# Reordering SyncE's transfers in a fused attention and mixture-of-experts layer: last group's strips first, next rows last

## The chip, the cores and the metric

The kernel runs on one core of a Trainium2 chip. The metric is device time in microseconds of one execution, the median over runs. Engines are named as the profile names them: PE (TensorE), PEld (its weight loads), DVE (VectorE), ACT (ScalarE), POOL (GpSimd) and SP (SyncE). SP computes nothing here: it issues DMA transfers, in one fixed order.

## The reference

One layer in float32 over x of 8 x 1024 tokens by 256 features:

```python
xn = layernorm(x)
x = x + attention(xn, w_qkv, w_out) + moe(xn, wg, w1, b1, w2, b2)
# attention: 16 heads of 64, causal, softmax over 1024 keys, then the output projection
qkv = einsum('bse,ehd->bshd', xn, w_qkv); q, k, v = split(qkv, 3, axis=-1)
logits = einsum('bqhd,bkhd->bhqk', q, k) / sqrt(64); probs = softmax(where(tril, logits, neg))
out = einsum('bshd,hde->bse', einsum('bhqk,bkhd->bqhd', probs, v), w_out)
# moe: 8 experts, top 2, 2048 slots per expert, relu(x w1 + b1) w2 + b2, weighted by the two gates
```

## The kernel before

The program has three stages: layernorm and router, the experts (results go to memory, one row for each slot), and from about 908 us of the profiled span on `attention_and_sum`, which also adds the experts' rows. Only that stage is changed.

**Units and steps.** The work of attention is 64 units: 8 batches (`BATCH`) of 8 pairs of heads (`PAIRS`). The order of each engine's work is written out by tables over 20 steps of a unit (`STEP_OF`, `ACT_STEP`, `DVE_STEP`, `RUN_STEP`, `POOL_AT`). In unit n, PE makes the scores of unit n in five rounds of query tiles (L1231), the projections of q and k for unit n+1 (L1142) and of v (L1157), the output projections "o0" to "o3" of unit n-1 (L1176), and the products of probabilities and values (L1263) in three runs: groups 0 and 1 at step 3 of unit n+1, group 2 at step 7 of unit n+1 (24 matmuls), group 3 at step 15 of unit n+1 (32 matmuls). A group is 256 query rows.

**Turning the probabilities.** Groups 0 and 1 are transposed by PE. For groups 2 and 3 DVE turns blocks of 32x32 into `squares` (L1398), and DMAs bring these blocks to their places in `pT`: 16 strips a group and unit, of which SP issues 12 (`place`, L1085: 96 KB each for group 2, 128 KB for group 3) and POOL 4 (`place_rest`, L1465, at steps 16 and 5). `place(n, g)` waits for the squares of the unit and for the PE run that read `pT` of this group a unit earlier. PE's run of group 2 or 3 waits for all 16 strips.

**The residual rows.** `res` holds the 1024 rows of a batch. It is filled from x (`refill`, L1094, four parts of 256 KB, one for each group), DVE adds each unit's output projection into it (L1381), POOL the rows of the experts (`total`, L1500, one tile of 128 rows a unit, at step 4), and at the end of a batch it is stored (`store`, L1089, four parts). Unit n with n % 8 == 0 is the change of batch: in it DVE adds the previous batch's last projections, o0 at step 6, o1 at 10, o2 at 12, and o3 at step 2 of the unit after. `store(b-1, g)` waits for that addition, `refill(b, g)` for the store of the same part. The new rows are first needed in unit n+1: part 0 by POOL's `total` at step 4, and by DVE's o0 at step 6.

**SP's other loads.** `load_w(n+2)` (L1073, two DMAs of 128 KB into `wr`) waits until POOL has split the weights of the unit before (`wlo`, L1448, step 1); POOL reads the new ones at step 1 of unit n+1 (L1441). The tile of tokens `xnt` (L1110, 128 KB) is loaded once PE has transposed the last one (step 1), and PE reads it at step 1 of unit n+1. `load_wv` (L1077, two DMAs of 128 KB into `wvr`) comes in even units once POOL has split the last ones (L1458, step 17), and is read two units later.

SP waits in order: an instruction behind a wait is issued after it, whatever it is for. Before, a unit's order is: `load_w`, `xnt`, strips of group 3 of unit n-1, [stores 0 to 2, refills 0 to 2], strips of group 2 of unit n, `load_wv`, [store 3, refill 3]; what stands in brackets is there at a change of batch alone, seven times in all.

Of the kernel before, what the change touches and what calls it, by code (L numbers as in the profile page):

```python
# [845 lines left out]
def attention_and_sum(nc, k, x, xn_dram, w_qkv, w_out, pick, y_dram, out, start):  # L846
# [7 lines left out]
    GROUPS = SEQ // GQ  # L854
# [77 lines left out]
    class Pieces:  # L932
        def __init__(self, sem_, own):
            self.sem, self.value, at = sem_, {}, 0
            for n in range(-1, UNITS + 1):
                for _, p in pieces(n):
                    at += own(p)
                    self.value[n, p] = at
# [5 lines left out]
    with ExitStack() as c:  # L944
# [45 lines left out]
        with ExitStack() as pre:  # L990
# [7 lines left out]
            @block.sync  # L998
            def _(e):
                e.dma_start(wo_raw, wov).then_inc(s_wo, 16)  # L1000
# [63 lines left out]
        def strip(g, a, b):  # L1064

            to, of = slice(b * BL, (b + 1) * BL), slice(a * BL, (a + 1) * BL)
            return wide[g][to, a].rearrange("p x r -> p (x r)"), sq[g][of, b].rearrange("p x k i -> p (x k i)")

        @block.sync
        def _(e):  # L1070
            def load_w(m):
                for c_ in range(MC):
                    e.dma_start(wr[:, 2 * c_:2 * c_ + 2], wv[m % PAIRS][:, c_, :, 0:2 * HDIM]).then_inc(wload.sem, 16)  # L1073

            def load_wv(m):
                for c_ in range(MC):
                    e.dma_start(wvr[:, c_], wvv[m % (PAIRS // 2)][:, c_, :, 2 * HDIM:]).then_inc(wvload.sem, 16)  # L1077

            def place(n, g):
                e.wait_ge(squared.sem, squared.at(n, 4 * g - 4))  # L1080
                if n > 0:
                    e.wait_ge(pv.sem, pv.at(n - 1, RUN_OF[g] + 1))
                for a in range(QUARTERS - 1):
                    for b in range(QUARTERS):
                        e.dma_start(*strip(g, a, b)).then_inc(placed[g].sem, 16)  # L1085

            def store(b, g):
                e.wait_ge(dve.sem, dve.at((b + 1) * PAIRS, f"o{g}"))
                e.dma_start(outv[:, b, 2 * g:2 * g + 2], res[:, 2 * g:2 * g + 2]).then_inc(stored[g].sem, 16)  # L1089

            def refill(b, g):
                if b > 0:
                    e.wait_ge(stored[g].sem, stored[g].at(b - 1, 16))
                e.dma_start(res[:, 2 * g:2 * g + 2], xv[:, b, 2 * g:2 * g + 2]).then_inc(rload[g].sem, 16)  # L1094

            e.dma_start(xnt[:], xnv[AHEAD]).then_inc(xload.sem, 16)
            load_w(1)
            load_wv(1)
            for n in range(UNITS):
                b, u = n // PAIRS, n % PAIRS  # L1100
                if n == 0:
                    e.wait_ge(s_wolo, 1)
                    for g in range(GROUPS):
                        refill(0, g)
                if n + 2 < UNITS:
                    e.wait_ge(wlo.sem, wlo.at(n, MC))
                    load_w(n + 2)
                if n + 1 + AHEAD < TILES:
                    e.wait_ge(filled.sem, filled.at(n, "xn"))
                    e.dma_start(xnt[:], xnv[n + 1 + AHEAD]).then_inc(xload.sem, 16)  # L1110
                if n > 0:
                    place(n - 1, 3)
                if b > 0 and u == 0:
                    for g in range(3):
                        store(b - 1, g)
                    for g in range(3):
                        refill(b, g)
                if n < UNITS - 1:
                    place(n, 2)
                if n % 2 == 0 and n // 2 + 2 < UNITS // 2:  # L1120
                    e.wait_ge(wvlo.sem, wvlo.at(n // 2, MC))
                    load_wv(n // 2 + 2)
                if b > 0 and u == 0:
                    store(b - 1, 3)
                    refill(b, 3)
            for g in range(GROUPS):
                store(BATCH - 1, g)
            for g in range(GROUPS):
                e.wait_ge(stored[g].sem, stored[g].at(BATCH - 1, 16))

        @block.tensor
        def _(e):
# [47 lines left out]
            def turn_p(n, name):  # L1180
                W, unit, at = work_bank(name), min(n, UNITS - 1), 0
                i, h, _, _ = TURNS[name][-1]
                e.wait_ge(scaled.sem, scaled.at(unit, SCALE_ORDER.index((i, h)) + 1))
                for i, h, k0, blocks in TURNS[name]:
                    for b in range(blocks):
                        cols = slice(OFFSET[i] + (k0 + b) * P, OFFSET[i] + (k0 + b + 1) * P)
                        ins = e.transpose(W[:, at * P:(at + 1) * P], room_of(unit, i, h)[:, cols], k["ident"][:])  # L1187
                        at += 1
                return ins

            def work(n, name):

                same = [(m, p) for m in (n - 1, n) if m >= -1 for _, p in pieces(m) if BANK_OF.get(p, 0) == BANK_OF[name]]
                same = same[:same.index((n, name))]
                if same:
                    m, p = same[-1]
                    if by_act(p):
                        e.wait_ge(act.sem, act.at(m, p))
                    if by_dve(p):
                        e.wait_ge(dve.sem, dve.at(m, p))  # L1200
                if name[0] == "p":
                    ins = project(n, name)
                elif name[0] == "v":
                    ins = values_of(n, name)
                elif name == "xn":
                    ins = turn_xn(n)
                elif name[0] == "t":
                    ins = turn_p(n, name)
                else:
                    ins = out_project(n, name)  # L1210
                ins.then_inc(filled.sem, 1)
# [359 lines left out]
```

## Time and profile before

| | us |
|---|---|
| median of 3 runs | 2915.8 (2915.28 to 2918.36) |
| the profiled execution's own time | 2915.7 |
| its span | 2913.9 |
| PE busy | 2814.5 (97% of the span) |
| DVE, ACT, POOL busy | 2084.7 (72%), 1699.7 (58%), 1723.0 (59%) |
| mean granted PE clock | 0.988 of full speed |
| chain that ended last: on PE | 66% of the span |

Times in rows are microseconds from the start of the span, unless marked ns. "x12" is a number of instructions; a time in square brackets is idle time of the engine before the instruction, with what ended it. "L1085" is a line of the kernel. A DMA's row on SP is the time to issue it, not to move its data; where a row gives the landing, that is from issue to the last byte. PEclk 1.00 is the full granted clock, the DMA share is the mean busy share of the core's 16 DMA engines.

### The profile page before, as it was taken

The numbers are of one execution on the slowest core, as the hardware profiler recorded it, in microseconds if no ns is written. First come the engines' busy times: TensorE is split into PE (matmuls) and PEld (weight loads), VectorE is DVE, ScalarE is ACT, GpSimd is POOL, SyncE is SP. The second block draws the span as 40 slices with busy tenths as digits, with TensorE's granted clock in tenths as the row PEclk, the third lists the DMA queues.
The fourth block names the chain that finished last, engine by engine and source line by source line (L and its number), as shares of the span: only waits on it lengthen the run. The fifth ranks groups of instructions, "written<-read, shape, count | busy, mean of one in ns | idle before, by whom it ended". The sixth has DMA issues, their size and how long they took to land.

```text
span 2913.9 us, 61264 instructions
## 1 busy us (share of the span) xinstructions
PE 2814.5 (97%) x21321; PEld 2284.1 (78%) x21321; DVE 2084.7 (72%) x4448; ACT 1699.7 (58%) x3934; POOL 1723.0 (59%) x2631
## 2 busy tenths in 40 slices
PE   5599999999998999999999999999999999999998
PEld 4489999899997777777777777777777777777776
DVE  7843444344434888888888888888888888888886
ACT  3454444445454666666666666666666666666664
POOL 3032122211212777777877877777777778777774
PEclk9799999999999999999999999999999999999999
DMA  7022212221212565665665565665665556556553
GB/s 241 29 82 75 69 52 83 76 68 47 82 54 74 141 158 144 163 154 145 168 150 145 147 170 147 157 166 142 157 164 151 149 146 176 141 145 183 136 134 93
DMA packets 248774, 371.58 MB, mean 128 GB/s; under 512 B 77392, under 2 KB 177744, under 8 KB 248480
## 3 DMA queue, kind: packets, MB, share of 16 engines
q1 hardware_dynamic: 216000, 276.31, 35.3%
q0 software_dynamic: 32480, 91.44, 11.7%
q8 instruction: 174, 2.85, 0.4%
q14 instruction: 120, 0.98, 0.1%
HBM read 102.80 MB, written 33.55 MB: 47 GB/s over the span
## 4 chain that ended last, share of the span: by engine, by line
PE 66%; DVE 1%; SPq 1%; DMA 0%; issue 0%; ACT 0%; POOL 0%; DVEq 0%; ACTq 0%
PE O L1263 18%; PE S L1231 16%; PE W L1142 12%; PE W L1157 7%; PE W L1176 7%; PE W L1187 6%; SPq L1085 1%; DVE pr L1355 0%; PE W L1165 0%; DMA pT<-squares 0%; DVE squares L1398 0%; ACT pr L1293 0%; DMA out<-res 0%; ACT pT L1283 0%; DVE res L1381 0%
## 5 line engine op out<-in xcount | busy, mean ns | idle before, releaser
L1436 POOL TENSOR_SCALAR pr<-pr,rinv 128x512 f32<-128x512 f32 (+7 forms) x1024 | 748.4, 744 | 399.7 <-DVE rinv L1361 398.6
L1293 ACT ACTIVATE pr<-pr,negm 128x512 f32<-128x512 f32 (+7 forms) x1024 | 787.3, 774 | 285.3 <-DVE negm L1355 285.3
L1355 DVE CUSTOM_DVE_ANT_0 pr<-S,late 128x512 f32<-128x512 f32 (+7 forms) x1024 | 717.0, 751 | 112.9 <-PE S L1231 112.9
L1263 PE MATMUL O<-pT,vv 128*64 128x256 f32 (+1 forms) x5120 | 541.3, 362 | 3.1 <-DMA pT<-squares 3.1
L1398 DVE STREAM_TRANSPOSE squares<-pr 128x640 f32<-128x640 f32 x504 | 494.8, 1020 | 0.0
L1263 PEld LDWEIGHTS O<-pT,vv 128*64 128x64 f32 x5120 | 346.4, 137 | 181.8 <-issue 20.4
L832 DVE TENSOR_TENSOR hl<-h,hh 128x512 fp32r<-128x512 f32 x256 | 192.3, 751 | 315.2 <-ACT hh L793 315.0
L789 ACT ACTIVATE h<-pH,b1c 128x512 f32<-128x512 f32 x256 | 175.9, 687 | 366.0 <-PE pH L719 334.1
L1283 ACT ACTIVATE pT<-W 128x512 f32<-128x512 f32 (+3 forms) x520 | 199.6, 437 | 215.8 <-PE W L1187 215.8
L731 PE MATMUL pY<-w2h,hh 128*128 128x256 f32 x1024 | 287.7, 281 | 2.5 <-DVE hl L832 2.5
L731 PE MATMUL pY<-w2l,hh 128*128 128x256 f32 x1024 | 289.1, 282 | 0.0
L731 PE MATMUL pY<-w2h,hl 128*128 128x256 f32 x1024 | 288.0, 281 | 0.0
L1465 POOL DMA_DIRECT2D pT<-squares x504 | 258.8, 521 | 0.3 <-issue 0.2
L1231 PE MATMUL S<-khf,qh 64*128 64x512 f32 (+2 forms) x1024 | 218.6, 422 | 3.6 <-DVE negm L1355 3.6
L1142 PE MATMUL W<-xnh,wh 128*128 128x512 f32 x512 | 215.1, 420 | 3.0 <-DVE klf L1389 1.5
L719 PE MATMUL pH<-xh,w1h 128*128 128x512 f32 x512 | 205.5, 401 | 4.2 <-DVE xl L804 2.6
L664 POOL COPY idx<-slot_token 128x4 uint32 (+1 forms) x30 | 8.8, 293 | 335.3 <-PE pX L705 335.3
L1142 PE MATMUL W<-xnl,wh 128*128 128x512 f32 x512 | 203.2, 397 | 0.0
L1142 PE MATMUL W<-xnh,wl 128*128 128x512 f32 x512 | 203.1, 397 | 0.0
L719 PE MATMUL pH<-xh,w1l 128*128 128x512 f32 x512 | 201.5, 394 | 0.0
L719 PE MATMUL pH<-xl,w1h 128*128 128x512 f32 x512 | 201.4, 393 | 0.0
L1381 DVE TENSOR_TENSOR res<-W,res 128x512 f32<-128x512 f32 x256 | 175.6, 686 | 35.6 <-PE W L1176 25.4
(176 smaller groups left out, 6479.6 us busy)
## 6 DMA issues: line engine op xcount, KB each, us to landing
pT<-squares SPq DMA_DIRECT2D x756, 128.0 KB
pT<-squares SPq DMA_DIRECT2D x756, 96.0 KB, 2.8
pT<-squares POOLq DMA_DIRECT2D x252, 128.0 KB
pT<-squares POOLq DMA_DIRECT2D x252, 96.0 KB, 3.0
y<-yb SPq DMA_DIRECT2D x128, 128.0 KB, 1.7
wr<-in_L_attn_w_qkv SPq DMA_DIRECT2D x128, 128.0 KB, 2.3
x<-in_L_attn_x SPq DMA_DIRECT2D x16, 512.0 KB, 8.9
xn<-xn SPq DMA_DIRECT2D x16, 512.0 KB, 4.4
```

The costliest lines, as they stand in the source:

```text
L719: ins = e.matmul(pH[hc % 4][:], w[par][:, m, ws], xx[q][:, m, :], start=(n == 0), stop=(n == 3 * MC - 1))
L731: ins = e.matmul(pY[t % 2][:], hs[q][:, hc, ts_], ws[par][:, hc, :], start=(hc == 0 and n == 0), stop=(hc == HC - 1 and n == 2))
L1142: ins = e.matmul(W, ws[:, 2 * m + of_k], xs[:, t0:t0 + HT, m, :], start=(i == 0), stop=(i == 3 * MC - 1))
L1157: ins = e.matmul(W[:, t * VW:(t + 1) * VW], xs[:, t0 + t, m, :], ws[:, m, :], start=(j == 0), stop=(j == len(terms) - 1))
L1176: ins = e.matmul(W[:, t * MODEL:(t + 1) * MODEL], os_[:, ts_], ws[:, of % PAIRS, :], start=(i == 0), stop=(i == 2))
L1231: ins = e.matmul(S[h][:, off + f * HALF:off + f * HALF + cols], t[hs, i * P:(i + 1) * P], u[f][n % 2][hs, 0:cols], start=(j == 0), stop=(j ...
L1263: ins = e.matmul(O[hs, o0 + a:o0 + GQ], vv[n // 2 % 2][:, kt, vs], turned_p, start=(kt == 0), stop=(kt == KT - 1))
L1293: e.activation(p, p, ACT.Exp, bias=negm[:, c0:c0 + 1], scale=-1.0, accum_out=rsum[:, c0:c0 + 1]).then_inc(expd.sem, 1)
L1355: e.tensor_tensor_reduce(room_of(n, i, h)[:, off:off + w], S[h][:, off:off + w], late[:, SEQ - w:], 1.0, -MASKED, ALU.add, ALU.min, negm[: ...
L1398: e.transpose(sq[g][:, :, 2 * h + i % 2, 0:KT, :], room_of(n, i, h)[:, OFFSET[i]:OFFSET[i] + KT * P].rearrange("p (k b i) -> p b k i", b=Q ...
L1436: e.tensor_scalar(p, p, rinv[:, c0:c0 + 1], 1.0, ALU.mult, ALU.mult).then_inc(scaled.sem, 1)
L1465: e.dma_start(*strip(g, QUARTERS - 1, b)).then_inc(pool_placed[g].sem, 16)
```

## The change

`place(n - 1, 3)` goes to the head of SP's loop. At a change of batch, refills 0 to 2 go behind the strips of group 2, and behind store 3, and store 3 and all four refills stand ahead of `load_wv`. No transfer is added, removed or resized, and no other engine's program is changed.

```diff
+                if n > 0:
+                    place(n - 1, 3)
                 if n + 2 < UNITS:
                     e.wait_ge(wlo.sem, wlo.at(n, MC))
                     load_w(n + 2)
                 if n + 1 + AHEAD < TILES:
                     e.wait_ge(filled.sem, filled.at(n, "xn"))
                     e.dma_start(xnt[:], xnv[n + 1 + AHEAD]).then_inc(xload.sem, 16)
-                if n > 0:
-                    place(n - 1, 3)
                 if b > 0 and u == 0:
                     for g in range(3):
                         store(b - 1, g)
-                    for g in range(3):
-                        refill(b, g)
                 if n < UNITS - 1:
                     place(n, 2)
+                if b > 0 and u == 0:
+                    store(b - 1, 3)
+                    for g in range(GROUPS):
+                        refill(b, g)
                 if n % 2 == 0 and n // 2 + 2 < UNITS // 2:
                     e.wait_ge(wvlo.sem, wvlo.at(n // 2, MC))
                     load_wv(n // 2 + 2)
-                if b > 0 and u == 0:
-                    store(b - 1, 3)
-                    refill(b, 3)
```

SP's queue at the first change of batch (unit 8 and the head of unit 9), before, from the refill of part 2 on. `pT2` and `pT3` are the places of groups 2 and 3, `s_stored3` is the landing of store 3:

```order
L1094 DMA res<-in_L0_attn_x 128x2x256 [waits s_stored2]
L1085 DMA pT2<-squares2 32x768 [waits s_pv,s_squared]
L1085 DMA pT2<-squares2 32x768 x11
L1077 DMA wvr<-in_L0_attn_w_qkv 128x4x64 [waits s_wvlo]
L1077 DMA wvr<-in_L0_attn_w_qkv 128x4x64
L1089 DMA out<-res 128x2x256 [waits s_dve]
L1094 DMA res<-in_L0_attn_x 128x2x256 [waits s_stored3]
L1073 DMA wr<-in_L0_attn_w_qkv 128x2x128 [waits s_wlo_a]
L1073 DMA wr<-in_L0_attn_w_qkv 128x2x128
L1110 DMA xnt<-xn 128x256 [waits s_filled]
L1085 DMA pT3<-squares3 32x1024 [waits s_pv,s_squared]
L1085 DMA pT3<-squares3 32x1024 x11
```

The same place of SP's queue with the change:

```order
L1085 DMA pT2<-squares2 32x768 [waits s_pv,s_squared]
L1085 DMA pT2<-squares2 32x768 x11
L1089 DMA out<-res 128x2x256 [waits s_dve]
L1094 DMA res<-in_L0_attn_x 128x2x256 [waits s_stored0]
L1094 DMA res<-in_L0_attn_x 128x2x256 [waits s_stored1]
L1094 DMA res<-in_L0_attn_x 128x2x256 [waits s_stored2]
L1094 DMA res<-in_L0_attn_x 128x2x256 [waits s_stored3]
L1077 DMA wvr<-in_L0_attn_w_qkv 128x4x64 [waits s_wvlo]
L1077 DMA wvr<-in_L0_attn_w_qkv 128x4x64
L1085 DMA pT3<-squares3 32x1024 [waits s_pv,s_squared]
L1085 DMA pT3<-squares3 32x1024 x11
```

Between the landing of store 3 and the strips of group 3 there stood refill 3, two `wr` loads and `xnt`; now there stand refill 3 and two `wvr` loads, and refills 0 to 2 are issued between store 3 and the wait for its landing.

An ordinary unit (the second after the change of batch), SP's queue before:

```order
L1073 DMA wr<-in_L0_attn_w_qkv 128x2x128 [waits s_wlo_a]
L1073 DMA wr<-in_L0_attn_w_qkv 128x2x128
L1110 DMA xnt<-xn 128x256 [waits s_filled]
L1085 DMA pT3<-squares3 32x1024 [waits s_pv,s_squared]
L1085 DMA pT3<-squares3 32x1024 x11
```

and with the change:

```order
L1085 DMA pT3<-squares3 32x1024 [waits s_pv,s_squared]
L1085 DMA pT3<-squares3 32x1024 x11
L1073 DMA wr<-in_L0_attn_w_qkv 128x2x128 [waits s_wlo_a]
L1073 DMA wr<-in_L0_attn_w_qkv 128x2x128
L1112 DMA xnt<-xn 128x256 [waits s_filled]
```

Twelve strips moved ahead of three loads.

## Rows read from the trace of the kernel before

**Rows 1.** The page: engines, slices of the span, costliest groups.
```profile
PE 2814.5 (97%) x21321; PEld 2284.1 (78%) x21321; DVE 2084.7 (72%) x4448; ACT 1699.7 (58%) x3934; POOL 1723.0 (59%) x2631
...
PE   5599999999998999999999999999999999999998
...
L1263 PE MATMUL O<-pT,vv 128*64 128x256 f32 (+1 forms) x5120 | 541.3, 362 | 3.1 <-DMA pT<-squares 3.1
```
**Rows 2.** Windows: busy time of a stretch, PEclk, DMA share, GB/s.
```profile
1010.40:1041.20 30.80, 30.80 (x248) 23.94 (x248) 25.77 (x58) 19.79 (x51) 23.26 (x37) 1.00 0.59 151
1195.00:1227.60 32.60, 30.84 (x247) 23.94 (x246) 25.81 (x58) 19.76 (x51) 23.55 (x38) 1.00 0.64 166
```
**Rows 3.** Waits of PE in 1160 to 1230, and in 1230 to 2850.
```profile
PE O L1263 <- DMA pT<-squares: 1.8, 1, 1.8
...
PE O L1263 <- DMA pT<-squares: 1.3, 1, 1.3
```
**Rows 4.** Timeline of SP at the first change of batch.
```profile
1172.83 7.95 SPq L1085 DMA_DIRECT2D pT<-squares  x12
1180.82 4.37 SPq L1089 DMA_DIRECT2D out<-res  x3
1185.43 3.49 SPq L1094 DMA_DIRECT2D res<-in_L_attn_x  x3
1189.02 7.59 SPq L1085 DMA_DIRECT2D pT<-squares  x12
1196.65 1.19 SPq L1077 DMA_DIRECT2D wvr<-in_L_attn_w_qkv  x2
1199.80 0.38 SPq L1089 DMA_DIRECT2D out<-res  x1
1204.11 0.37 SPq L1094 DMA_DIRECT2D res<-in_L_attn_x  x1
1204.53 0.98 SPq L1073 DMA_DIRECT2D wr<-in_L_attn_w_qkv  x2
1205.56 0.47 SPq L1110 DMA_DIRECT2D xnt<-xn  x1
1206.12 8.44 SPq L1085 DMA_DIRECT2D pT<-squares  x12
```
**Rows 5.** Chain of waits at PE's first wait in this stage.
```profile
1213.32 0.59 SPq L1085
1213.92 0.04 issue
1213.96 4.79 DMA pT<-squares
1218.76 0.04 issue
1218.80 1.29 PE O L1263 x9
```
**Rows 6.** Timeline of SP at the second, third and sixth change of batch.
```profile
1448.14 0.38 SPq L1089 DMA_DIRECT2D out<-res  x1
1451.36 0.37 SPq L1094 DMA_DIRECT2D res<-in_L_attn_x  x1
...
1696.04 0.38 SPq L1089 DMA_DIRECT2D out<-res  x1
1698.25 0.37 SPq L1094 DMA_DIRECT2D res<-in_L_attn_x  x1
...
2439.76 9.95 SPq L1085 DMA_DIRECT2D pT<-squares  x12
```
**Rows 7.** Timeline of PE: run of group 3 after the sixth change.
```profile
2452.75 1.08 PE L1263 MATMUL O<-pT,vv 128*64 128x256 f32 x8
```
**Rows 8.** Windows of 2 us after the first change's store 3, as rows 2.
```profile
1202.00:1204.00 2.00, 2.00 (x21) 1.86 (x18) 2.00 (x7) 0.20 (x1) 1.55 (x4) 1.00 0.04 8
1206.00:1208.00 2.00, 2.00 (x24) 1.42 (x22) 1.13 (x3) 1.38 (x6) 2.00 (x6) 1.00 0.83 247
1210.00:1212.00 2.00, 2.00 (x13) 1.69 (x13) 1.63 (x7) 2.00 (x6) 1.53 (x3) 1.00 1.04 270
```
**Rows 9.** Timeline of POOL and DVE after the first change of batch.
```profile
1205.00 0.73 POOL L1500 TENSOR_TENSOR res<-res,yg 128x256 f32<-128x256 f32 x1
...
1205.85 0.69 DVE L1381 TENSOR_TENSOR res<-W,res 128x512 f32<-128x512 f32 x1 [0.66 <-POOL res L1500]
1207.03 0.18 DVE L1361 RECIPROCAL rinv<-rsum 128x4 f32<-128x4 f32 x1 [0.48 <-ACT pr L1293]
1207.59 0.42 DVE L1405 TENSOR_TENSOR ol<-O,oh 128x256 fp32r<-128x256 f32 x1 [0.39 <-ACT oh L1324]
1208.88 0.96 DVE L1355 CUSTOM_DVE_ANT_0 pr<-S,late 128x768 f32<-128x768 f32 x1 [0.86 <-PE S L1231]
```
**Rows 10.** SP, DVE and POOL two units after the first change, and a unit later.
```profile
1234.78 0.89 SPq L1073 DMA_DIRECT2D wr<-in_L_attn_w_qkv  x2
1236.28 23.25 SPq L1085 DMA_DIRECT2D pT<-squares  x24
...
1232.34 2.36 DVE L1398 STREAM_TRANSPOSE squares<-pr 128x1024 f32<-128x1024 f32 x2
...
1262.75 0.39 POOL L1441 TENSOR_SCALAR wr<-wr 128x256 f32<-128x256 f32 x1
```
**Rows 11.** DMA issues of the page: kind, count, size, median time to landing.
```profile
wr<-in_L_attn_w_qkv SPq DMA_DIRECT2D x128, 128.0 KB, 2.3
...
res<-in_L_attn_x SPq DMA_DIRECT2D x32, 256.0 KB, 3.0
out<-res SPq DMA_DIRECT2D x32, 256.0 KB, 3.7
```

## The prediction

> **What bounds the kernel now.** I read the page first. PE is busy 97% of the span, and from the fourteenth slice on, the attention stage, its digit is 9 in nearly all [rows 1]. Then the windows: an ordinary unit of this stage takes 30.80 us and PE is busy for all 30.80 of it, at the full granted clock [rows 2]. A transfer can cost time here only where PE waits for it. So the third view is PE's own waits in the part of the stage that repeats. Between 1160 and 2850 us there are two, both of the run of values (L1263) for strips of pT, 1.8 and 1.3 us [rows 3]; the page's total for that line is the same 3.1 [rows 1]. The unit with the first wait lasts 32.60 us with 30.84 busy [rows 2]: the wait is time lost, not time shifted. These 3.1 us are all that a better order of SP's queue can return in that part, 0.11% of 2915.7. The start of the stage and the last unit have PE waits as well, but for other engines, and SP's order there hardly changes.
>
> Both waits stand one unit after a change of batch. The timeline of SP tells why [rows 4]. Store 3 is issued at 1199.80; SP then waits for it to land before it may issue refill 3 (1204.11), and only then come two wr loads, xnt, and at 1206.12 the twelve strips of group 3. The chain of waits at PE's stall goes through these strips: the last is issued at 1213.32 and waited for until 1218.76 [rows 5]. The wait of SP for the store was 4.3 us at the first change, 3.2 at the second (1451.36 less 1448.14) and 2.2 at the third (1698.25 less 1696.04) [rows 4, 6]. PE lost 1.8, 1.3 and nothing. The slow stores make the stall, and the reader should see that the change leaves this wait ahead of group 3's strips.
>
> **The change, part by part.**
>
> *Ordinary units.* Strips of group 3 now need only the squares, which end at 1234.70 (1232.34 and 2.36), instead of standing behind a load that began at 1234.78; they start about 1.5 us earlier (1236.28 less 1234.78) [rows 10]. PE waits for none of them, so this gives 0. The price is later loads: wr goes out some 8 us later (twelve strips took 7.95 [rows 4]), at about 1243, lands 2.3 later [rows 11], and POOL reads it at 1262.75 [rows 10], 17 us after that. xnt is read by PE at the same step of the unit as wr by POOL, so its room is about the same. Cost 0. If that room were gone, POOL's split and then PE's projections would be late, in 56 units.
>
> *Group 2's strips at a change.* They stood behind three refills and started at 1189.02 [rows 4]; the refills waited for store 2. Now they start as soon as the squares are done. PE's two waits are both for group 3's strips [rows 3, 5], none is for group 2's, so I book 0.
>
> *Group 3's strips after a change.* This is the term that counts. From the landing of store 3 to the first strip it took 1206.12 less 1204.11 = 2.01 us. That was refill 3, 0.37; two wr, 0.98; xnt, 0.47; and gaps [rows 4]. Now it is refill 3, 0.37, and two wvr, 1.19, with three gaps of 0.04 to 0.05: 1.69. The load of wvr came in from the other side of the wait, and takes back most of what wr and xnt gave: 0.32 us remain. In bytes, 256 KB stand ahead of the strips in place of 384 KB. The DMA engines are full behind them (share 1.04, 270 GB/s), so 128 KB fewer could be worth 131072 B / 270 GB/s = 0.5 us more [rows 8]. Against it, wvr moves in runs of 64 elements and wr in runs of 128, by the shapes in SP's queue, and twice the runs may cost as much; I take 0 and keep 0.5 as an end. Gain: 0.32 at each of the two stalls, so **0.6 us**; with 0.5 more at each, 1.6; and 3.1 at most.
>
> *Refills 0 to 2 behind store 3.* They are now issued, 3 x 256 KB, while SP waits for the store. Between 1202 and 1204 the DMA engines are at a share of 0.04 [rows 8], so they fill a hole. What I cannot read is whether they delay the store's landing: no row here has loads queued behind a store that SP waits for. From below the delay is 0, or slightly negative, as wvr no longer stands ahead of it; from above it is the time of all three at the full rate, 786432 B / 270 GB/s = 2.9 us. I take 0, because the store is issued first and a 256 KB store landed after 2.2 us at the third change [rows 6], when the three could barely have been issued (0.4 us each) and read.
>
> The Trainium skill, in "DMA: Bandwidth & Descriptors", section "Queues, rings and completion order", says that each DMA engine takes a ring's descriptors in order and that the semaphore's increment lands after every earlier write of that engine. By this rule the delay is 0 and the sum is the one below; by the upper bound of the row it would be the first rival. No run here shows it yet.
>
> *Refill 0 is later.* It goes out at about 1200.2 in place of 1185.43. POOL's total, which reads it, begins at 1205.00 [rows 9]; refills land after 3.0 us in the median [rows 11], so at 1203.2, or with the store's 256 KB ahead (1.0 us at 270 GB/s) at 1204.2. Cost 0, with a margin of 0.8 us. Were it late, DVE's o0 (1205.85) would wait for POOL, and DVE has to spare the time until 1208.88 less its work of 0.69, 0.18 and 0.42: 1.7 us [rows 9]. Parts 1 to 3 are needed later, at steps 10, 12 and 22.
>
> **Sum.** 2915.7 for the profiled execution, less 0.6, is 2915.1; the median of the runs stands 0.1 above that execution, so 2915.2. I forecast **2915.2 us**.
>
> **Rivals.**
>
> *The store waits for the loads behind it* (slower). If the three refills hold store 3 back by d, group 3's strips start d - 0.32 later. At the two stalls that is paid in full. At the other five there is some room: from the end of the last strip's issue to PE's run was 4.24 us where PE waited (1218.80 less 1214.56) [rows 4, 5], but only 3.04 without a wait at the sixth change (2452.75 less 2449.71) [rows 6, 7]; so the room is between 0 and about 1.4 us, and I use 0.7. For d = 2.9: 2 x 2.6 + 5 x (2.6 - 0.7) = 14.7 us slower, 2930. It decides from d of about 1.6: 2 x 1.3 + 5 x 0.6 = 5.6. For it: SP's wait for stores varied from 2.2 to 4.3 us, so something does delay them. Against it: the order of issue. Chance of a result over 0.2% slower by this: 0.06; of a smaller loss (d about 1, 2 x 0.7 = 1.4 us slower, 2917.2): 0.12.
>
> *Refill 0 comes too late* (slower). If it lands l after 1205.00, each of seven changes costs l - 1.7. For a landing 3 us late, 9 us, 2925. It needs a landing of 8 us from issue, and the median is 3.0. Chance 0.02.
>
> *Full recovery.* If the 128 KB fewer and the empty queue ahead of the store work together, both stalls go: 2915.8 less 3.1, 2912.7. For it: at the second change 0.8 of 1.3 us is in sight. Against it: the long wait for the store itself is untouched. Chance 0.15.
>
> *The profile misses time* (faster). The 3.1 us are of one execution, and of three runs one took 2918.4; if the usual execution loses more at the changes than the profiled one, removing it could give over 5.8. Nothing in the trace speaks for it. Chance 0.02.
>
> **How the numbers follow.** The forecast's own case has the rest, 0.63, and lies between 2914 and 2916. About 0.2%, 5.8 us, is what a measurement of this kernel can tell from no change. Forecast, full recovery and the small loss are all within it: 0.90. Slower 0.06 + 0.02 = 0.08. Faster 0.02. For the range, the low end is full recovery with the lowest of the runs (2915.28 less 3.1): 2912.2. The high end takes in the small loss and the spread of the runs upward (2917.2 and 2.2, which is most of 2918.36 less 2915.8): 2919.4. Left out are the two slower rivals and a part of the tails.
>
> **What would show it.** Right: two or fewer waits of L1263 for strips, summing to 1 to 2.7 us; from the landing of store 3 to group 3's first strip 1.7 us; refills 0 to 2 issued within 1.3 us behind store 3; POOL's total still some 5.2 us behind store 3; ordinary units at 30.80. Wrong: SP's wait for store 3 longer than 2.2 to 4.3 us, waits of L1263 after more than two changes, DVE's o0 waiting longer than 0.66 for POOL, POOL or PE waiting for wr, wvr or xnt.

## The result and the profile after

The changed kernel takes **2922.0 us** (median of 22 runs, 2913.8 to 2931.6); the kernel before, run beside it, 2916.7 (22 runs, 2911.0 to 2924.1). The ratio is 1.0019, 95% interval 1.001 to 1.0028: slower by 2.9 to 8.2 us, where 0.6 us faster was forecast, and above the range's end of 2919.4.

The page of the changed kernel (behind SP's loop its lines are numbered one lower than before; xnt's is L1112):

```profile
PE 2819.0 (96%) x21321; PEld 2285.7 (78%) x21321; DVE 2083.7 (71%) x4448; ACT 1698.7 (58%) x3934; POOL 1722.0 (59%) x2631
...
L1262 PE MATMUL O<-pT,vv 128*64 128x256 f32 (+1 forms) x5120 | 544.7, 364 | 6.5 <-DMA pT<-squares 6.5
```

The idle time of the runs of values has doubled, from 3.1 [rows 1] to 6.5 us. The waits of PE between 1160 and 2850 us, where before there were two, of 1.8 and 1.3 us [rows 3]:

```profile
PE O L1262 <- DMA pT<-squares: 6.5, 7, 2.0
```

Seven waits, one behind each change of batch, and nothing else. The timeline of SP at the first and at the third change, to be held against [rows 4, 6]:

```profile
1191.09 7.51 SPq L1085 DMA_DIRECT2D pT<-squares  x12
1202.34 0.38 SPq L1089 DMA_DIRECT2D out<-res  x1
1202.76 4.10 SPq L1094 DMA_DIRECT2D res<-in_L_attn_x  x4
1206.91 1.02 SPq L1077 DMA_DIRECT2D wvr<-in_L_attn_w_qkv  x2
1208.02 8.69 SPq L1085 DMA_DIRECT2D pT<-squares  x12
...
1701.32 0.38 SPq L1089 DMA_DIRECT2D out<-res  x1
1701.74 2.13 SPq L1094 DMA_DIRECT2D res<-in_L_attn_x  x4
1703.92 1.02 SPq L1077 DMA_DIRECT2D wvr<-in_L_attn_w_qkv  x2
1705.03 8.37 SPq L1085 DMA_DIRECT2D pT<-squares  x12
```

SP is not late. At the third change the strips start 3.71 us behind the issue of store 3 (1705.03 less 1701.32), where it was 4.21 before. At the first it was 6.32 (1206.12 less 1199.80) and is now 5.68. And yet the data come later. The run that needs them began at 1713.2 at the third change before, and PE did not wait for it (its first eight matmuls):

```profile
L1263 PE MATMUL O<-pT,vv x8: 379/379/430, 1713.2 to 1713.9; 128*64 128x256 f32 x8
```

and the end of the chain of waits at the same change now:

```profile
1712.81 6.30 DMA pT<-squares
1719.11 0.04 issue
1719.15 3.02 PE O L1262 x25
```

The last of SP's strips is waited for 6.30 us from its issue; POOL's four had been issued by 1708.7. (Before, the last was issued at 1708.22 and was there by 1713.2, so it took 5.0 us or less.) Of the 6.5 us, 4.0 stand at the first two changes, where 3.1 stood before, and 2.5 at the five that had no wait. Now the windows of 2 us from about store 3 of the third change on (length, PEclk, DMA share, GB/s), first before:

```profile
1696.00:1698.00 2.00, 1.00 0.38 131
1698.00:1700.00 2.00, 1.00 0.27 78
1700.00:1702.00 2.00, 1.00 0.86 257
1702.00:1704.00 2.00, 1.00 0.87 247
1710.00:1712.00 2.00, 1.00 0.58 121
```

and after:

```profile
1701.30:1703.30 2.00, 1.00 0.53 164
1703.30:1705.30 2.00, 1.00 0.94 289
1705.30:1707.30 2.00, 1.00 1.05 308
1707.30:1709.30 2.00, 1.00 1.13 232
1715.30:1717.30 2.00, 1.00 1.02 212
```

A share can come out a little above 1, since a packet's whole time counts in the window in which it starts. Before, the DMA engines are mostly free for the first 4 us, and at 1710 the work thins out. After, they are full from 2 us behind the store on and still full 14 to 16 us behind it. The landings say the same. These are the two wvr loads of the third change, before and after:

```profile
DMA to landing us min/median/max: 2.7/2.8/2.8
DMA to landing us min/median/max: 4.0/5.0/6.1
```

Refill 3 takes 2.6 us before and 5.1 after. When the strips begin at 1705.03, refills 1 to 3 and both wvr loads have still to land.

Waits are not all. Windows of PE around the first change's wait (length, PE busy, PEclk, DMA share, GB/s):

```profile
1216.00:1221.70 5.70, 3.70 (x25) 1.00 1.02 228
1221.70:1225.10 3.40, 3.40 (x18) 0.51 0.24 55
1225.10:1240.00 14.90, 14.90 (x123) 1.00 0.34 97
```

and the run in its timeline:

```profile
1221.58 5.15 PE L1262 MATMUL O<-pT,vv 128*64 128x256 f32 x32 [2.00 <-DMA pT<-squares]
```

PE waited 2.00 us, and right behind that it ran for 3.4 us at the lower of its two levels (1.2 in place of 2.4 GHz, granted clock 0.51). The run of 32 matmuls took 5.15 us in place of 3.46: another 1.7 us. Before, no such stretch follows the waits of 1.8 and 1.3 us, and in the change none follows the second change's wait, which was 2.01 us long.

### The profile page after: what moved, and what is told of

The parts are those of the page before. It is cut to its first block, busy times and chain, and to the rows that moved or that the text cites. A ratio compares the mean times of both kernels' runs of the same rounds, so it can differ in the third digit from the quotient of the medians.

```text
span 2923.6 us, 61264 instructions
## 1 busy us (share of the span) xinstructions
PE 2819.0 (96%) x21321; PEld 2285.7 (78%) x21321; DVE 2083.7 (71%) x4448; ACT 1698.7 (58%) x3934; POOL 1722.0 (59%) x2631
## 4 chain that ended last, share of the span: by engine, by line
PE 61%; DVE 2%; SPq 2%; DMA 2%; issue 1%; ACT 0%; POOL 0%; DVEq 0%; ACTq 0%
PE O L1262 17%; PE S L1230 15%; PE W L1141 11%; PE W L1156 6%; PE W L1175 6%; PE W L1186 5%; SPq L1085 2%; DMA pT<-squares 1%; DVE pr L1354 1%; DVE squares L1397 1%; DMA out<-res 1%; PE W L1164 0%; SPq L1077 0%; DVE res L1380 0%; DVE ql L1388 0%
```

## The experiments

The theory after the result (called A, or the backlog, in the expectations): refills 0 to 2, 768 KB, moved to just ahead of group 3's strips, fill the DMA engines, and the strips land late however early they are issued. Rivals: the place at the head of the loop hurts by itself (B), or the two wvr loads between refill 3 and the strips do (C).

**Only the strips to the head.**

```diff
+                if n > 0:
+                    place(n - 1, 3)
                 if n + 2 < UNITS:
...
-                if n > 0:
-                    place(n - 1, 3)
```

> Only the strips of group 3 go to the head of SP's loop; stores, refills and wvr stay where they were. Theory A (the transfers of refills 0 to 2 fill the DMA engines ahead of group 3's strips): no late refills, and neither wr nor xnt ahead of the strips, so they start about 0.4 us behind the landing of store 3 and PE's waits for strips between 1160 and 2850 us go from 3.1 to 0 or under 0.5. Theory B (the head position hurts by itself, in every unit, through later wr and xnt loads): ordinary units longer than 30.81 us or waits of POOL for wr, and a time near that of the whole change, +5 us. Theory C (it is SP's two wvr loads between refill 3 and the strips): like A here.

2913.3 us (12 runs; before 2916.3), ratio 0.9984 (0.9974 to 0.9994). PE waits for no strip at all. SP at the first change:

```profile
1204.31 0.37 SPq L1094 DMA_DIRECT2D res<-in_L_attn_x  x1
1204.78 8.04 SPq L1085 DMA_DIRECT2D pT<-squares  x12
```

B falls: this half of the change is a gain. All 3.1 us of waits are gone, and the medians differ by 3.0 (by the interval, 1.7 to 7.6).

**Only the rows moved.** The change, with `place(n - 1, 3)` left behind wr and xnt.

> Only the rows move (place of group 2's strips, store 3, refills 0 to 3, then wvr), and the strips of group 3 stay behind wr and xnt. Theory A: 1.5 us more of issue and 384 KB more ahead of the strips than in the whole change, with the same late refills: PE waits at all seven changes, 2 to 3.5 us each, 14 to 20 us in all, time +12 to +20 us against the kernel before. Theory B: no harm, waits near 3.1. Theory C: waits also above the 6.5 of the whole change, by the 1.5 us of issue at each of the seven.

2932.7 us (5 runs), ratio 1.0052 (1.0037 to 1.0066), and these waits:

```profile
PE O L1262 <- DMA pT<-squares: 16.5, 7, 3.2
```

As A said; but C had foretold nearly the same (1.5 us more at each of the seven), so this run speaks only against B. This half costs some 16 us against before, and the other takes 11 of them back.

**Refills 0 to 2 back in their place.**

```diff
                     for g in range(3):
                         store(b - 1, g)
+                    for g in range(3):
+                        refill(b, g)
...
                     store(b - 1, 3)
-                    for g in range(GROUPS):
-                        refill(b, g)
+                    refill(b, 3)
```

> The whole change, but refills 0 to 2 back where they were, ahead of group 2's strips. Store 3, refill 3, wvr, then group 3's strips as in the change. Theory A: the DMA engines have their hole behind store 3 again, and the strips start 1.7 us behind its landing: waits of PE at two changes or fewer, 1.5 to 2.8 us in sum, time within 1 us of before. Theory C (wvr): waits stay at all seven changes, 6.5 us. Theory B: time stays at +5.

2916.3 us (12 runs), ratio 1.0002 (0.9991 to 1.0012). Waits:

```profile
PE O L1263 <- DMA pT<-squares: 2.5, 2, 2.2
```

C by itself falls: wvr stands ahead of the strips here too, and the waits are about those of before. The loss needs the late refills.

**Thin refills.** The order and the number of transfers of the change, fewer bytes. The kernel leaves out 224 of the 256 columns of these rows, so its output is not the layer's:

```diff
+                cols = slice(0, 32 if b > 0 and g < 3 else MODEL)
-                e.dma_start(res[:, 2 * g:2 * g + 2], xv[:, b, 2 * g:2 * g + 2]).then_inc(rload[g].sem, 16)
+                e.dma_start(res[:, 2 * g:2 * g + 2, cols], xv[:, b, 2 * g:2 * g + 2, cols]).then_inc(rload[g].sem, 16)
```

> The whole change, with refills 0 to 2 at a change of batch cut to 32 of the 256 columns (32 KB in place of 256 KB each), so the residual rows of batches 1 to 7 are not all loaded: the order and the number of issues are those of the change, the bytes are not. Theory A: waits of PE fall from 6.5 us at seven changes to 1 to 3 us at two. Were it the issues or the order and not the bytes: 6.5 stays.

2916.7 us (12 runs), ratio 1.0001 (0.9992 to 1.001), and

```profile
PE O L1263 <- DMA pT<-squares: 3.4, 3, 1.5
```

The waits fall to about those of before, a little above what was expected (1 to 3 us at two changes; here three). So it is the data of the three refills, not their issue or their place in SP's order, that wvr needs beside it to make the loss.

**wvr ahead of store 3 again**, refills late as in the change.

> The whole change, but the two wvr loads back ahead of store 3. Backlog theory: the late refills are still there, but 256 KB and 1.2 us of issue less stand ahead of the strips; the waits of 2.1, 2.1, 0.7, 0.2, 0.9, 0.5, 0.5 us (by the longer units) lose about 1.2 each, so 1.5 to 2.5 us at two to four changes are left. If the refills alone did it, whatever wvr does: 5 us or more left.

2915.7 us (11 runs; before 2917.1), ratio 0.9995 (0.9985 to 1.0006).

```profile
PE O L1262 <- DMA pT<-squares: 2.6, 2, 1.5
```

The waits are just above what the backlog gave (1.5 to 2.5), and C has a share after all: with neither the late refills nor wvr ahead of the strips the waits are 0, with wvr alone 2.5, with the refills alone 2.6, with both 6.5. Two groups of loads that do little alone fill the engines together, and taking either back undoes the loss. The two waits here are at the second and the fourth change, 1.0 and 1.5 us, and the change itself lost only 0.2 at the fourth; so bytes ahead of the strips give the sum, not each wait.

**Refills 0 to 2 in the gap.** Behind the strips of group 2, ahead of store 3, in SP's idle 3 us.

> The whole change, but refills 0 to 2 directly behind the strips of group 2, in the 3 us in which SP waits for DVE before store 3. Backlog theory: by the time of group 3's strips their data have passed, so the waits are those of refills back in their old place, 2 to 3 us at two changes; if store 3 lands later behind them, up to 1 us more at each change.

2922.2 us (12 runs), ratio 1.0018 (1.0007 to 1.003). This missed: I had expected waits of 2 to 3 us, with up to 1 us more at each change if store 3 came later.

```profile
PE O L1264 <- DMA pT<-squares: 6.2, 5, 1.8
```

SP at its third change shows what went wrong:

```profile
1690.86 1.64 SPq L1094 DMA_DIRECT2D res<-in_L_attn_x  x3
1694.32 0.38 SPq L1089 DMA_DIRECT2D out<-res  x1
1698.12 0.37 SPq L1094 DMA_DIRECT2D res<-in_L_attn_x  x1
```

Store 3 landed 3.8 us from its issue, in place of 2.2 before and in the change. Behind loads issued 2.3 to 3.5 us ahead of it, it came 1.6 us later here, and 0.4 to 1.2 us later at the four changes that follow, but not at the first two (4.2 and 3.2 us, as before). In the change three loads are issued right behind it, and at the third change it lands after 2.2 as before.

**Refill 3 behind the strips as well**, on top of the strips at the head:

```diff
                 if n > 0:
                     place(n - 1, 3)
+                if b > 0 and u == 1:
+                    refill(b, 3)
...
                     store(b - 1, 3)
-                    refill(b, 3)
```

> The strips of group 3 at the head of the loop, rows and wvr as in the kernel before, and refill 3 behind these strips, so that no wait for a store stands ahead of them. Backlog theory: the strips start when their squares are done, some 3 us earlier than with the head position alone, so PE never waits for strips; since PE's waits were 0 with the head position alone too, the time is that one's within 1.5 us, about 3 us under the kernel before.

**2911.0 us** (11 runs, 2909.7 to 2915.0; before 2917.1), ratio 0.9979 (0.997 to 0.9988), the fastest. SP at the first change:

```profile
1198.13 0.38 SPq L1089 DMA_DIRECT2D out<-res  x1
1200.40 8.65 SPq L1085 DMA_DIRECT2D pT<-squares  x12
1209.10 0.59 SPq L1094 DMA_DIRECT2D res<-in_L_attn_x  x1
```

No wait for a store stands ahead of the strips any more. In the profiled executions neither this kernel nor the one with the head position alone has a wait for strips between 1160 and 2850 us, so the profile gives no reason for the 2 us between their medians, and the intervals overlap. The spans of the two profiled executions differ by 2.2 us as well (2908.9 and 2911.1), but that is there before this part of the stage begins: the first run of values starts at 949.1 and at 951.5.

**All refills behind the strips.** As the last, with refills 0 to 2 taken there too.

> The strips of group 3 at the head, and all four refills behind them, one unit after the change of batch. The DMA engines then take the strips first and PE's run of group 3 never waits for them, but refill 0 is issued some 13 us behind store 3, lands 3 to 4 us later, and POOL's total, due 5.2 us behind store 3, waits some 11 us for it, with POOL's scales and its own four strips behind it. By the room of 1.7 us that I gave this wait in the prediction, 9 us are lost at each change: about 60 us slower. If POOL and DVE have more room than I read, less.

2953.9 us (4 runs), ratio 1.0128 (1.0113 to 1.0143): 37 us slower, where 60 were expected. POOL, and PE's waits:

```profile
1209.86 0.72 POOL L1500 TENSOR_TENSOR res<-res,yg 128x256 f32<-128x256 f32 x1 [7.70 <-DMA res<-in_L_attn_x]
```

```profile
PE W L1187 <- DVE res L1381: 32.7, 7, 5.0
```

The refills were issued 9.8 us behind store 3, not 13, so POOL waited 7.70 and not 11; PE then waited 4.7 on average, so the room is 3.0 us and not 1.7. This is my second rival, made to happen: refill 0 may be late, but by no more than 3 us. And again the clock, window as above:

```profile
1212.10:1215.50 3.40, 3.40 (x14) 0.53 0.90 240
```

At each of the seven changes the clock is at half behind this wait of 4.6 to 5.0 us; at the seventh it falls within it and stays there for 6.8 us.

**The same two kernels again**, one profile each.

> The whole change unaltered, a second profile. Its first had 6.5 us of waits for strips at seven changes, and two stretches of 3.4 us at half the granted clock in the attention stage, one of them right behind its longest wait. If waits are the mechanism they repeat: 5.5 to 7.5 us at six or seven changes. If the half-clock stretches come of waits of 2 us and more, one or two stand within a few us of the waits at the first two changes again.

> A third profile of the whole change: as the second, waits 5.5 to 7.5 us; a half-clock stretch behind a wait of 2 us in one of the two further profiles or in both.

> The kernel before, a second profile: waits for strips 2 to 4 us at two or three changes, no half-clock stretch between 1000 and 2850 us, since no wait reaches 2 us.

> The kernel before, a third profile: as the second, 2 to 4 us at two or three changes and no half-clock stretch between 1000 and 2850 us.

Their waits for strips, the change twice and then the kernel before twice, and the windows behind the first change's wait in the two of the change:

```profile
PE O L1262 <- DMA pT<-squares: 6.1, 5, 2.4
```

```profile
PE O L1262 <- DMA pT<-squares: 6.3, 7, 2.1
```

```profile
PE O L1263 <- DMA pT<-squares: 3.2, 3, 1.8
```

```profile
PE O L1263 <- DMA pT<-squares: 2.0, 2, 1.4
```

```profile
1220.50:1223.90 3.40, 3.34 (x16) 0.51 0.33 81
```

```profile
1218.20:1221.60 3.40, 3.40 (x18) 0.54 0.40 98
```

The sums are as expected, one of the change's with five waits where six or seven were expected, and the half-clock stretch is there both times, at the first change alone: behind the second change's waits, 2.3 and 1.6 us, the clock stayed full. Near the end of the stage (about 2867 us) one of the two of the kernel before had such a stretch as well, and so had all three profiles of the change between 2870 and 2893. It stands there behind one of two waits of about 1.85 us that every profile of both kernels has, so the length of the wait does not decide it. The change moves nothing there, so whether its greater frequency is chance stays open.

## Why the prediction was wrong

- **What bounds the kernel, and what can be returned: right.** PE's two waits, 3.1 us, are all there is in this part. The head position alone returns them: 2913.3. The rival *Full recovery* gave 2912.7 for the whole change; one half of the change alone gets there.
- **Ordinary units: right.** Outside the seven waits PE waits for nothing between 1160 and 2850 us in the change, and POOL never waits for wr.
- **Group 3's strips: right about the issue, wrong about what follows.** At six of the seven changes the strips start 0.3 to 0.6 us earlier from the store's issue (5.68 for 6.32 at the first change). I booked this as a gain of 0.32 at each stall; from the store's landing on it was 0.5 (1.53 us in place of 2.01, where I forecast 1.69), as the two wvr took 1.02 us to issue and not 1.19. Measured: waits of 6.5, 6.1 and 6.3 us in place of 3.1, 3.2 and 2.0, so 3.5 us more on average.
- **The step that failed** is "Refills 0 to 2 behind store 3 ... so they fill a hole". I asked only whether they delay the store, and never what they do to the strips behind them. The hole was read at the first change, where SP waits 4.3 us for its store; at the third it waits 2.2 us, and three refills at 270 GB/s need 2.9. My count of "256 KB ahead of the strips in place of 384" began at the landing of the store. From the issue of store 3 on it is 1280 KB (four refills and wvr) in place of 640 (refill 3, wr, xnt); the 640 KB more are 655360 B / 270 GB/s = 2.4 us of a full engine, against 0.5 of earlier start. The two free windows of the third change held 2.7 us of engine time before (0.62 and 0.73 of 2 us each), and the change leaves 1.1 of it unused (0.47 and 0.06), so only some 1.6 us of the work found room; as an estimate, the rest is 0.8 us. PE's run began 17.83 us behind the issue of store 3, where before it began at 17.16 (1713.20 less 1696.04) without waiting: 0.67 us later. With thin refills this term is gone and so is the loss.
- **The first rival's mechanism did not come.** Store 3 lands 2.2 us from its issue at the third change with three loads behind it, as it did with none, and so it does at the four changes after it in all three profiles of the change. The Trainium skill, "DMA: Bandwidth & Descriptors", section "Queues, rings and completion order", says that a DMA engine takes a ring's descriptors in order. The trace agrees with it here: what was issued behind the store did not hold it back. The slower side came by another way, which none of the rivals named. The room I gave the five changes without a wait (0 to 1.4 us) was the right thing to ask for, of the wrong cause.
- **The second rival did not come**: POOL's total starts 5.2 us behind store 3 as before (1207.53 less 1202.34). It was closer than forecast, though: refill 0 landed 4.3 us from its issue at the first change, about 0.5 us ahead of the total, where I had a margin of 0.8. Its room was 3.0 us, not 1.7.
- **No term for the clock.** In three of three profiles of the change the first wait, 2.0 to 2.4 us, was followed by 3.4 us at half the clock, a loss of half of it, 1.7 us; in none of the three of the kernel before was it. With the 3.5 us of waits that makes 5.2, and the medians differ by 5.3. That this fits so well is in part luck. The three profiled executions of the change are longer than the three of before by 7.8 us on average (spans of 2923.6, 2921.7 and 2919.8 for 2913.9, 2913.8 and 2913.9). The rest of these 7.8 is the stretch near the end, in three of three in place of one of three (1.1 us), some 1.0 us that is there before the first run of values, near 950 us, and 0.5 whose place is not known.

## What to carry to other kernels

A transfer moved out of one gap of an in-order queue lands in another. For each move, add up the bytes that are in flight when the transfer that someone waits for is issued, and hold them against the free share of the DMA engines there at every repetition, not at one: the gap may be shorter at the next. Where two halves of a change can be run alone, run them: here one was worth 3 us and the other cost 16.

## What the runs showed of the hardware

- A 256 KB store landed 2.2 us from its issue with 768 KB of loads issued right behind it, and 3.8 us with the same loads issued 2.3 to 3.5 us ahead of it (third change; 2.5 to 3.3 at the four after it, and no later than before at the first two).
- With the DMA engines full (share 1.0 and more), the two 128 KB loads of wvr took 4.0 and 6.1 us to land at the third change, in place of 2.8.
- The first change's store 3 took 3.7 to 4.3 us in all fourteen profiles, with quite different loads around it, the second's 2.9 to 3.8, and from the third on it was 2.1 to 2.3 in all but the one with refills ahead of it: it goes with the batch. Why is open.
- A wait of PE can cost more than its length: behind waits of 2.0 to 2.4 us at the first change the granted clock was at half for 3.4 us in all three profiles of the change, and behind all seven waits of 4.6 to 5.0 us with all refills behind the strips. But it stayed full behind one of 2.2 us with the refills back and behind one of 2.95 us with only the rows moved, and it fell in one of three profiles of the kernel before behind a wait of 1.85 us. So the length alone does not tell; what else does is open.
